# The middle step's first convolution as a four-row transform of x, with two planes made on GpSimd

## The reference

```python
for _ in range(3):                        # three steps, H_STEP = 1/3
    t = relu(conv3x3(x, w1) + b1)         # first convolution of the step
    x = x + H_STEP * (conv3x3(t, w2) + b2)  # second convolution
x = relu(x)

qkv = einsum('oc,bchw->bhwo', qkv_w, x)   # 8 heads of 8 channels
k, v = ln(k), ln(v)                       # each head's 8 channels, ddof=1
kv = einsum('bhnd,bhne->bhde', k, v) / N  # N = 4096 pixels
ret = einsum('bhnd,bhde->bhne', q, kv) + x
u = gelu(einsum('oc,bchw->bohw', o1_w, ret))
out = gelu(einsum('oc,bchw->bohw', o2_w, u) + x)
```

## Time and profile before

| | |
|---|---|
| median of 3 runs | 1490.61 us (1490.42 to 1491.71) |
| profiled execution, own time | 1491.92 us |
| its span, first to last instruction | 1490.2 us |
| busy TensorE / VectorE / ScalarE / GpSimd | 1379.1 / 903.1 / 557.6 / 89.8 us |
| mean granted TensorE clock | 0.97 |

### The profile page before, as it was taken

How to read it: one execution, slowest core, us unless ns; L and a number is a source line. 1 busy time by engine, 2 the same in 40 slices (tenths; PEclk the granted TensorE clock), 3 DMA queues, 4 the chain that set the end, 5 groups by cost and what they waited for, 6 DMA issues and landing times.

```text
span 1490.2 us, 35900 instructions
## 1 busy us (share of the span) xinstructions
PE 1379.1 (93%) x16533; PEld 794.6 (53%) x16533; DVE 903.1 (61%) x1041; ACT 557.6 (37%) x610; POOL 89.8 (6%) x115
## 2 busy tenths in 40 slices
PE   7799999999999999999999999999999999988764
PEld 3456565565455646465464654556454664645442
...
PEclk9899999999999999999999999999999999989778
...
GB/s 133 107 10 2 118 1 31 31 92 27 30 144 2 118 1 85 89 41 80 15 127 34 83 36 29 145 2 118 1 71 103 31 89 12 77 88 1 29 87 57
DMA packets 88082, 88.50 MB, mean 59 GB/s; under 512 B 71292, under 2 KB 71292, under 8 KB 87932
## 3 DMA queue, kind: packets, MB, share of 16 engines
...
...
## 4 chain that ended last, share of the span: by engine, by line
PE 81%; DVE 8%; ACT 4%; issue 3%; DMA 2%; SPq 2%; POOL 0%; ACTq 0%; DVEq 0%
PE ps L765 49%; PE ps L789 19%; PE ps L819 4%; PE ps L830 4%; PE ps L855 2%; PE ps L864 2%; DMA xs<-in_x 2%; SPq L331 1%; DVE rstd L658 1%; ACT g L494 1%; DVE kv L663 1%; DVE q L583 1%; ACT g L506 1%; DVE v L600 1%; ACT kv L485 1%
## 5 line engine op out<-in xcount | busy, mean ns | idle before, releaser
L765 PE MATMUL ps<-xs,w_t 64*64 64x512 f32 x6912 | 778.6, 598 | 17.6 <-issue 6.5
L765 PEld LDWEIGHTS ps<-xs,w_t 64*64 64x64 f32 x6912 | 334.9, 134 | 412.9 <-issue 380.3
L789 PE MATMUL ps<-v,fw 64*64 64x256 f32 x6912 | 396.9, 381 | 6.9 <-ACT m L455 5.3
L789 PEld LDWEIGHTS ps<-v,fw 64*64 64x64 f32 x6912 | 291.9, 133 | 106.3 <-issue 19.2
L428 ACT ACTIVATE t<-ps,b_col 128x1024 f32<-128x1024 f32 x96 | 108.4, 1129 | 447.9 <-PE ps L765 447.9
L583 DVE TENSOR_TENSOR q<-t 128x2112 f32<-128x2112 f32 x48 | 112.9, 2352 | 107.9 <-ACT t L428 103.9
L404 POOL DMA_DIRECT2D xs<-dx x96 | 83.2, 968 | 1340.6 <-DVE dx L645 1330.9
L651 DVE TENSOR_REDUCE rstd<-g 128x128 f32<-128x1024 f32 x64 | 77.9, 1217 | 131.5 <-ACT g L494 131.5
L819 PE MATMUL ps<-kvw,y 64*128 64x128 f32 x1024 | 78.3, 296 | 30.7 <-ACT g L494 17.8
L485 ACT ACTIVATE kv<-ps 128x1024 f32<-128x1024 f32 x64 | 65.6, 1026 | 107.1 <-PE ps L819 100.7
L690 DVE TENSOR_TENSOR y<-ps,xs 128x1024 f32<-128x1024 f32 x32 | 39.0, 1222 | 96.7 <-PE ps L864 91.8
...
## 6 DMA issues: line engine op xcount, KB each, us to landing
...
xs<-in_x SPq DMA_DIRECT2D x128, 128.0 KB, 4.4
...
b_col<-in_L_conv_b SPq DMA_DIRECT2D x4, 0.2 KB, 3.4
...
```

What stands on the lines that cost most here:

```text
L765: last = mm(to[CH * side:CH * side + CH, BANK * p:BANK * p + BANK], w1_t[half, tap, :], tile[half, rows, c:c + COLS], start=tap == 0, stop ...
L789: last = mm(to[CH * i:CH * i + CH, at:at + SPAN], fw[rows, product, c, :], v[half % V_RING][rows, tiles, place, i, c:c + COLS], start=c == ...
```

## The change

The second `conv0` (s = 1) of pairs 1 to 7 becomes `fast0`. Its input x goes through the transform that t goes through for `conv1`; the six products use w1's transformed weights `fw0`, which are made on VectorE in iteration 1; the result is combined straight into `t`, and ScalarE applies bias and relu in place (`fill_t`). A `fast0` has 6 units of 24 matmuls over 256 columns, in gaps 28 to 33; gaps 34 and 35 keep their numbers and hold no unit. For every transform, of t as of x, planes V1 and V2 are now made on GpSimd (`pair_planes`). `V_RING` is 4 instead of 3, and `dx` has one buffer instead of two. `TRANSFORMS`, `LATE`, `LAST` and `FINAL` are rewritten.

```diff
-X_RING, V_RING = 3, 3
+X_RING, V_RING = 3, 4
+FAST = {(a, 1) for a in range(1, IMAGES // 2)}
...
-TRANSFORMS = {5: (0, 0), 10: (0, 1), 27: (3, 0), 31: (3, 1), 34: (4, 0), 40: (4, 1)}
+TRANSFORMS = {4: (2, 0, 0), 14: (2, 0, 1), 23: (4, 0, 0), 24: (4, 0, 1),
+              27: (5, 0, 0), 29: (5, 0, 1), 35: (1, 1, 0), 40: (1, 1, 1)}
...
-        dx = [sb(f"dx{h}", [P, 2, 4 * TILES, PADDED]) for h in range(HALVES)]
+        dx = sb("dx", [P, 2, 4 * TILES, PADDED])
+        fw0 = sb("fw0", [P, 2, 6, K, CH])
...
+            def pair_planes(half):
+                to = v[half % V_RING].rearrange("p c k i w -> p c k (i w)")
...
+                pool.wait_ge(steps_made, 2 * half + 2)
+                nc.gpsimd.tensor_tensor(to[:, :, 0], eo[:, :, 1, :], eo[:, :, 0, :], ALU.add)
+                nc.gpsimd.tensor_tensor(to[:, :, 1], eo[:, :, 1, :], eo[:, :, 0, :], ALU.subtract
+                                        ).then_inc(v_paired, 1)
...
+            def fill_t(unit, h):
+                entry = ENTRY[(*unit[:3], h)]
+                act.wait_ge(combined, entry + 1)
+                rows = t[:, 16 * h + 1:16 * h + 17, :, 1:COLS + 1].rearrange("p j i w -> p (j i) w")
+                if h == HALVES - 1:
...
+                nc.scalar.activation(rows, rows, ACT.Relu, bias=b1_col[:, :]).then_inc(t_made, 1)
...
+            def steps_of_x(a, s, h, combines):
...
+                    for k in range(HALVES):
+                        dve.wait_ge(x_added[k], 32 * (FIRST[a, s - 1] + 1))
+                to = q.rearrange("p r (i w) -> p r i w", i=2)
+                vec.tensor_tensor(to[:, :, 0, :], tile[:, at + 2:at + 18, :], tile[:, at:at + 16, :], ALU.subtract)
...
-                if n:
-                    dve.wait_ge(x_added[h], 32 * n)
+                if unit[0] == CONV1 and n + h:
+                    dve.wait_ge(x_added[1 - h], 32 * (n + h))
...
-                dve.wait_ge(v_made, transformed)
+                dve.wait_ge(v_paired, transformed)
...
+                    pe.wait_ge(v_made, half + 1)
+                    pe.wait_ge(v_paired, half + 1)
```

The attention's steps of one iteration around the new convolution, before and now:

```diff
-    24: (steps(OUTER, 4) + steps(NORMALISE, 6) + steps(OUTER, 5) + steps(NORMALISE, 7) + steps(OUTER, 6, 7)),
-    31: (steps(DOWN, 0) + steps(FINISH, 0)),
-    32: (steps(UP, 1)),
-    33: (steps(DOWN, 1)),
-    34: (steps(UP, 2) + steps(DOWN, 2) + steps(FINISH, 1)),
-    35: (steps(UP, 3) + steps(FINISH, 2)),
-    36: (steps(FINISH, 3) + steps(DOWN, 3)),
+    28: (steps(OUTER, 6) + steps(NORMALISE, 7) + steps(OUTER, 7) + steps(FOLD, 0, 1, 2)),
+    29: (steps(FOLD, 3)),
+    30: (steps(UP, 0)),
+    31: (steps(DOWN, 0)),
+    32: (steps(FINISH, 0) + steps(UP, 1)),
+    34: (steps(DOWN, 1) + steps(UP, 2) + steps(FINISH, 1) + steps(UP, 3) + steps(DOWN, 2) + steps(FINISH, 2)
+        + steps(DOWN, 3) + steps(FINISH, 3)),
```

More of the change, by code:

```diff
@@ L75 @@
     for _nth, _phase in enumerate(phases(_it)):
-        if _nth in (0, 3, 4):
+        if _nth in (0, 3, 4) and _phase and _phase[0] == FAST0:
+            for _u in range(2 * BLOCKS):
+                GAPS.append((_it, _gap + _u, (*_phase, _u) if _u < HALVES * PARTS else None, 1))
+            _gap += 2 * BLOCKS
+        elif _nth in (0, 3, 4):
             for _b in range(BLOCKS):
@@ L587, in transform_t @@
-                if combined:
-                    dve.wait_ge(dx_made, combined)
-                vec.scalar_tensor_tensor(eo[:, :, :, :], centre, -4.0, ahead, ALU.mult, ALU.add).then_inc(t_read, 1)
+                if phase[0] == FAST0:
+                    steps_of_x(*phase[1:], h, combines)
+                else:
+                    steps_of_t(phase[1:], h, combines)
                 step = q.rearrange("p (c r) w -> p c r w", r=4)
                 if half >= V_RING:
-                    done = CONV1S[(half - V_RING) // HALVES] + (PARTS * ((half - V_RING) % HALVES) + PARTS - 1,)
+                    *before, side = ENTRIES[half - V_RING]
+                    done = (*before, PARTS * side + PARTS - 1)
@@ L708, in _ @@
                     make_rest()
+                if (it, gap) == (1, 7):
+                    transform_w1()
                 for a, s in todo(it, gap):
```

287 lines of the change are left out of this document (190 added, 97 removed).

## The result

| | before | after |
|---|---|---|
| median | 1490.92 us (1490.42 to 1491.71, 4 runs) | 1583.84 us (1582.12 to 1591.04, 4 runs) |
| profiled execution, its span | 1491.92 us, 1490.2 us | 1591.04 us, 1589.1 us |
| busy TensorE / VectorE / GpSimd | 1379.1 / 903.1 / 89.8 us | 1347.4 / 1156.0 / 325.3 us |
| mean granted clock | 0.97 | 0.91 |

The ratio is 1.063, with an interval of 1.0597 to 1.0667: slower by 6.3%. The forecast was 1530 us with a range up to 1562. The direction came out, the size did not. The profiled execution is 7 us above its median, so the 99 us between the two spans are some 93 between the medians.

The account below looks back on a forecast made before the run. TensorE, busy 1379 of 1490 us, was taken as the bound. A round: -4.4 us plus 10.4 for GpSimd, +6.0; six +36, iteration 1 +4: 1530 us against the median, own range 1505 to 1562, full range 1440 to 1562.

Parts of the forecast that it names:

- the walk of the round without GpSimd: Steady round of TensorE, GpSimd's planes costing nothing: 15.7 us saved against waits and clock, -4.4 us a round.
- rival 1: GpSimd beside VectorE costs nothing: -26 us, 1464 us against the median; chance 0.24.
- GpSimd's hold: GpSimd's V1 and V2 delay VectorE's two-input instructions in full: 2.0 us a transform, ends 0 and 2.7.
- The places: Gap 6 1.2 us, gap 17 1.6, NORMALISE 7 ahead of OUTER 7 5.6, the copy `gw` 2.0.
- +10.4 us a round: Sum of GpSimd's delay at four places of a steady round, turning -4.4 into +6.0 us.
- the 2.0 for `gw`: The copy `gw`, which UP 0 waits for, comes 2.0 us later through GpSimd's delay.
- Rival 4: VectorE becomes the bound at 2.7 us a transform, 151 us of a round, late waits: 1565 or more; chance 0.08.
- +4: Iteration 1's share of the sum, beside +36 us for six rounds.
- I take 0: Iteration 1: its 15.7 us saving set against w1's transform, 9.4 us idle at `fill_t` and 4 for the clock.
- iterations 8 and 9, "0": Iterations 8 and 9, like iteration 0, hold no `fast0` and were charged 0.
- the clock of gap 34: UP and DOWN at 1.98 instead of 1.08 us and slow units behind: up to 5.5 us, 3.5 taken.
- the forecast's own case: The 1530 us forecast with its own range 1505 to 1562 us; chance 0.50.

Follow-up runs that it names:

- e2b: The changed kernel with GpSimd's two instructions for V1 and V2 cut to 8 of 528 elements each, same waits, results wrong: 1477.4 us, ratio 0.991.
- e4: The changed kernel with GpSimd memsets writing constants over V1 and V2 in place of the sum and the difference: 1476.5 us, one run.
- e11: The changed kernel with matmuls without use (fillers) ahead of TensorE's waits in iterations 2 to 7: 1560.5 us, ratio 1.048.
- e10: The changed kernel with V1 and V2 on VectorE, two dx and three V buffers, fast0 kept: 1512.6 us, ratio 1.016.
- e5b: The changed kernel, planes still on GpSimd, with two dx buffers again and three V buffers for four: 1576.2 us, ratio 1.056.
- e3: The kernel before with nothing changed but V1 and V2 of its transforms on GpSimd: 1498.9 us, ratio 1.004.
- e15: The kernel of e14 with V1 and V2 on GpSimd as in the change: 1555.5 us, ratio 1.044.
- e14: The kernel of e10 with the second transform of t at gap 30 and the steps of gaps 32 to 34 reordered: 1491.9 us, ratio 1.001.

## Why the prediction was right and wrong

**Right: the walk of the round without GpSimd.** 171.2 us predicted, 172.0 measured in e2b in the mean and 171.0 in the round shown, gap 34 at 8.4 us idle for 9.6, its groups at 1.98 us, the clock at 4.3 us for 3.5. That it fits to 1 us is in part luck: the idle time came out 1.5 us below the walk's (12.4 for 5.6 + 0.9 + 1.1 + 8.4 - 2.1 = 13.9), the busy time 1.3 above it (158.6 for 157.3). Without GpSimd's hold the change would have been faster than before, as rival 1 said, but by 13.5 us (e2b) and not by 26.

**Right: the mechanism and price of GpSimd's hold.** 2.0 us a transform predicted, 2.2 measured. Of the condition that I took from the rows, two inputs on VectorE and reading on GpSimd, e4 shows the second half; the first is not tested, since every instruction that was held has two inputs. The places: ahead of OUTER 7 5.4 us for 5.6, ahead of the unit of gap 9, whose PSUM region is drained behind DEVIATION, 1.3 for 1.2, at gap 17 2.3 for 1.6. UP 0 did not wait for `gw` (predicted 2.0 more), since VectorE was the first there and GpSimd waited. Instead UP 1 waits 0.8 us (0.2 in e2b), and PROJECT 0 waits 2.85 us (1.06 in e2b), which I had not seen. That the idle time came to 10.0 us for 10.4 is luck in part: one place too many and two too few balance.

**Wrong: the sum of that term, +10.4 us a round, which is 15.1 (e2b against the change), 28 us in six rounds.** It held waits alone. In "Four places feel the 2.0 us" no place has a price for the clock, though the walk before had one for gap 34 and named rows 9 for it. GpSimd's planes add 10.0 us of idle time, as forecast, and 6.3 us of slow matmuls on top: 1.7 behind PROJECT 0 and 3.9 from OUTER 7 to the unit behind the fold. The stretch from OUTER 7 to DOWN 1 grew by 3.5 us through them, where I had only the 2.0 for `gw`. The fillers of e11 took back 1.5 of them; how many of the slow matmuls ahead of OUTER 7 only fill a wait for VectorE stays open. Rival 4 had the words for it ("clock losses at each new wait"), with a chance of 0.08 and the wrong bound: VectorE is busy for 145.9 of 187 us in a round, its holds included (129.2 in e2b, for 129.7 in the forecast), and never became the limit by its busy time.

**Wrong: iterations 0 and 1, "+4".** They cost 22.0 us. By the profiled executions the one `dx` is 13 to 16 of them (e10 and e5b), GpSimd's planes 6 to 9 (e3, and e15 against e14), and fast0 itself gains 2 (e10). I had priced the one `dx` at 2.2 us from its 8.4 us of latency, in a steady round, where VectorE's other work covers most of it. In iteration 1 there is no attention, nothing covers it, and the wait stands ahead of a transform that TensorE needs. My "I take 0" for iteration 1's own work hid that.

**Wrong: iterations 8 and 9, "0".** From iteration 7 to the end it is 15.9 us more, one round's 12.2 among them, so 3.7 us are left. They hold transforms with GpSimd's planes, too, and new tables; no run separates the two.

Against the spans: predicted 40, measured 99. The rounds were 36 and are 73, the start 4 and is 22, the tail 0 and is 4.

**The range** ended at 1562, with 1505 to 1562 for the forecast's own case. It took GpSimd's price up to 2.7 us and the clock of gap 34 up to 5.5 us, and both came out inside. What it had no bound for was more waits, each with its own clock, and iteration 1.
